# A transformer block on one core: ScalarE copies 192 score pieces as bf16, VectorE joins them three at a time

## The reference, cut to what matters

```
mod = (silu(c) @ wmod).reshape(4, 6, 1, 256)          # sa, ca, ga, sb, cb, gb
h = layernorm(x) * (1 + ca) + sa                      # x: 4 x 1024 x 256
q, k, v = 16 heads of 16 from h @ w_qkv.T + b_qkv
attn = softmax(q @ k.T / 4);  vals = attn @ v
x = x + ga * (vals @ w_o.T + b_o)
h = layernorm(x) * (1 + cb) + sb
scores = sigmoid(h @ gate.T); pick 6 of 32 experts out of 4 of 8 groups; weights = 2.5 * normalised scores
x = x + gb * (sum over chosen experts of weight * expert(h) + shared_expert(h))
```

## Time and profile before

| | |
|---|---|
| timed runs | 1418.58 us median of 3 (1416.19 to 1419.35) |
| span of the profiled execution | 1412.3 us |
| TensorE matmul busy | 1342.8 us (95%) |
| VectorE busy | 1134.9 us (80%) |
| ScalarE busy | 753.7 us (53%) |
| attention steps | 152.3 to 880.3 us |

### The profile page before, as it was taken

One profiled execution on the slowest core, in us unless ns is written; L12 is line 12 of the kernel. 1 busy time (PEld: TensorE's weight loads), 2 busy tenths in 40 slices (PEclk: granted clock), 3 DMA queues, 4 the chain that ended last, 5 costly groups with the idle time before them and its releaser, 6 DMA issues.

```text
span 1412.3 us, 30839 instructions
## 1 busy us (share of the span) xinstructions
PE 1342.8 (95%) x8191; PEld 672.8 (48%) x8192; DVE 1134.9 (80%) x2823; ACT 753.7 (53%) x1155; POOL 606.9 (43%) x782
## 2 busy tenths in 40 slices
PE   7997999999999999999999999999999999999895
PEld 4552222332333323323333232568788888888551
DVE  7886999999999999999999994566566656656588
ACT  3762477676767676777677768113343433334100
POOL 4000113143644534636346357527755555655300
PEclk9997799999999999999999999999999999999999
DMA  6898355533546345444464355947766665666698
GB/s 218 260 270 216 93 171 133 121 85 83 125 126 156 91 121 149 132 96 107 125 170 117 105 155 176 274 136 234 231 199 206 202 183 177 180 179 178 238 344 337
DMA packets 216958, 243.55 MB, mean 172 GB/s; under 512 B 93948, under 2 KB 181500, under 8 KB 216736
## 3 DMA queue, kind: packets, MB, share of 16 engines
q1 hardware_dynamic: 189328, 166.42, 43.6%
q0 software_dynamic: 21776, 68.07, 13.4%
q10 hardware_dynamic: 5760, 7.87, 1.7%
HBM read 133.98 MB, written 108.28 MB: 172 GB/s over the span
## 4 chain that ended last, share of the span: by engine, by line
PE 71%; DVE 13%; DMA 4%; issue 1%; SPq 1%; ACT 1%; POOL 0%; DVEq 0%; POOLq 0%
PE psO L1174 14%; PE ex_psGU L1682 13%; PE psE L1161 13%; PE psM L1151 9%; DVE piece_max L1048 9%; PE ex_psY L1697 7%; PE ex_psX L1671 3%; PE psM L505 2%; PE ex_psA L1691 2%; PE psGU L1495 1%; DMA wide<-results 1%; PE co_psS L1951 1%; PE late_psGU L1931 1%; PE late_psX L1942 1%; PE psM L524 1%
## 5 line engine op out<-in xcount | busy, mean ns | idle before, releaser
L1048 DVE TENSOR_REDUCE piece_max<-psM 128x1 f32<-128x512 f32 x1024 | 641.9, 680 | 27.3 <-PE psM L1151 24.0
L1115 ACT ACTIVATE wide<-psE 128x1024 f32<-128x1024 f32 x512 | 496.8, 1021 | 206.2 <-PE psE L1161 204.1
L1151 PE MATMUL psM<-wide 48*128 48x512 bf16 x1024 | 324.0, 395 | 19.9 <-DVE piece_max L1048 11.7
L1161 PE MATMUL psE<-wide 49*128 49x512 bf16 (+1 forms) x2048 | 328.7, 380 | 3.2 <-DMA wide<-maxima 2.8
L1763 POOL DMA_INDIRECT results<-vals_inv,places x223 | 213.9, 959 | 150.5 <-DVE vals_inv L1749 86.4
L1174 PE MATMUL psO<-wide 128*32 128x512 f32 x2048 | 273.6, 606 | 0.6 <-ACT wide L1115 0.6
L1151 PEld LDWEIGHTS psM<-wide 48*128 48x128 bf16 x1024 | 78.1, 93 | 348.1 <-DVE piece_max L1048 277.3
L1682 PE MATMUL ex_psGU<-wide,ex_xT 128*128 x892 | 231.3, 382 | 0.8 <-ACT ex_xT L1714 0.7
L1161 PEld LDWEIGHTS psE<-wide 49*128 49x128 bf16 (+1 forms) x2048 | 117.6, 95 | 92.3 <-issue 8.7
L1682 PEld LDWEIGHTS ex_psGU<-wide,ex_xT 128*128 128x128 f32 x892 | 152.1, 190 | 14.6 <-issue 2.3
L1714 ACT ACTIVATE ex_xT<-ex_psX 128x256 f32<-128x256 f32 x223 | 85.3, 383 | 121.3 <-PE ex_psX L1671 118.5
(11 more groups left out here) (281 smaller groups left out, 1262.8 us busy)
## 6 DMA issues: line engine op xcount, KB each, us to landing
wide<-qk_parts SPq DMA_DIRECT2D x384, 64.0 KB
wide<-results SPq DMA_DIRECT2D x16, 1536.0 KB, 9.5
rows<-lists SPq DMA_DIRECT2D x112, 160.0 KB
h2Ts<-lists SPq DMA_DIRECT2D x111, 160.0 KB
qk_parts<-parts SPq DMA_DIRECT2D x32, 384.0 KB, 3.1
xin<-in_x_dram SPq DMA_DIRECT2D x16, 512.0 KB, 4.2
v_values<-vst SPq DMA_DIRECT2D x32, 256.0 KB, 3.5
wide<-v_values SPq DMA_DIRECT2D x16, 512.0 KB
```

What stands on the lines that cost most here:

```text
L1048: v.tensor_reduce(piece_max[:, qh, (x * PAIRS + h) * KT // QH + qt, kh:kh + 1], bank_of("piece", PIECES * group + n), AX.X, ALU.max, negat ...
L1115: nc.scalar.activation(probs[:, step % 2, 2 * pair:2 * pair + 2], psE[:, pair], ACT.Exp, scale=HD ** -0.5).then_inc(exp_ok, 1)
L1151: nc.tensor.matmul(bank_of(*user), qa[g][rows, h, qt * P:(qt + 1) * P], ka[g][rows, h, kh * 512:(kh + 1) * 512], start=True, stop=True).th ...
L1161: mm = nc.tensor.matmul(psE[:, pair, x], k[g][part, pair, kt * P:(kt + 1) * P], q[g][part, pair, qh * 512:(qh + 1) * 512], start=(q is qa) ...
```

## The change

ScalarE now reads six pieces of each half of 32, 192 in all: always p2, in the steps that are 0, 1, 2, 4, 5 and 6 of the half (`held_at`; step 0 of a half is step 5 modulo 8). `hold` copies such a piece as bf16 to SBUF, at the end of ScalarE's step. VectorE leaves these pieces out and works on three copies at a time in `join`: elementwise maximum of 3x256 elements (level 0), of 3x128 (level 1), of 3x64 (level 2), and a reduction of 3x64 to three maxima (level 3). The first three are joined in step 4 of the half, the second three in the first step of the next half, where `finish` now stands too, behind p1 and ahead of p3. `divide` moves from step 5 to step 6 of a group. The maxima are stored with one transfer and loaded with one, and `max_d` has a part for each half.

```diff
-DIVIDE = 5
+DIVIDE = 6
+    HELD_PIECE, HELD_STEPS, TRIPLE = 2, (0, 1, 2, 4, 5, 6), 3
+    FIRST_JOINED = 4
...
+        held = [of.bitcast(BF16)[:, 0:TRIPLE * 512].rearrange("p (n k) -> p n k", n=TRIPLE)
+                for of in (env.act_s[:].rearrange("p m t -> p (m t)"),
+                           env.x2[:, TPC * LAST:].rearrange("p i d -> p (i d)"))]
...
+        def held_at(n):
+            return n % 4 == HELD_PIECE and n // 4 % STEPS_HALF in HELD_STEPS
...
             def store_max(k):
-                at = COLS * (k % QH)
                 sp.wait_ge(max_ready, k + 1)
-                for n in range(P // 32):
-                    sp.dma_start(env.max_d[at:at + COLS, n], neg_max_t[32 * n + at:32 * n + at + COLS, :]
-                                 ).then_inc(max_stored, 16)
+                sp.dma_start(env.max_d[k % QH].rearrange("c n r -> n c r"), neg_max_t[:]).then_inc(max_stored, 16)
...
+            def join(half, triple, level):
+                of = held[triple]
+                if level < 3:
+                    width = 256 >> level
+                    if level == 0:
+                        dve.wait_ge(piece_held, TRIPLE * (2 * half + triple + 1))
+                    else:
+                        chain.ready()
+                    chain.then(v.tensor_tensor(of[:, :, 0:width], of[:, :, 0:width], of[:, :, width:2 * width], ALU.max))
+                else:
+                    chain.ready()
+                    at = HELD_STEPS[TRIPLE * triple]
+                    v.tensor_reduce(piece_max[:, half % QH, at:at + TRIPLE, HELD_PIECE // 2], of[:, :, 0:64], AX.X, ALU.max,
+                                    negate=True).then_inc(joined, 1)
+
+            def piece_or_join(group, n):
+                if not held_at(n):
+                    piece_maximum(group, n)
+                p, r = n // 4 % STEPS_HALF, n % 4
+                if p == FIRST_JOINED:
+                    for level in ((0,), (1, 2), (3,), ())[r]:
+                        join(QH * group + n // HALF_PIECES, 0, level)
+
+            def finish_half(k, n):
+                if n == 0:
+                    join(k, 1, 0)
+                elif n == 1:
+                    for level in (1, 2, 3):
+                        join(k, 1, level)
+                elif n == 2:
+                    finish(k)
...
                 for n in range(4):
                     beside(step, n)
                     if group < NGR:
-                        piece_maximum(group, first + n)
-                if group < NGR and (first + 4) % HALF_PIECES == 0:
-                    finish(QH * group + first // HALF_PIECES)
+                        piece_or_join(group, first + n)
+                    done = QH * group + first // HALF_PIECES - 1
+                    if first % HALF_PIECES == 0 and 0 < done < QH * NGR:
+                        finish_half(done, n)
...
+            def hold(group, n):
+                at = held_before(PIECES * group + n)
+                triple, slot = divmod(at, TRIPLE)
+                act.wait_ge(piece_done, PIECES * group + n + 1)
+                if slot == 0:
+                    wait(act, joined, triple - 1)
+                nc.scalar.activation(held[triple % 2][:, slot], bank_of("piece", PIECES * group + n), ACT.Copy
+                                     ).then_inc(piece_held, 1)
...
+                to, first = pieces_for(step)
+                for n in range(first, first + 4):
+                    if to < NGR and held_at(n):
+                        hold(to, n)
...
-                if c == "piece":
-                    pe.wait_ge(piece_read, w + 1)
+                if c == "piece" and held_at(w % PIECES):
+                    pe.wait_ge(piece_held, held_before(w + 1))
+                elif c == "piece":
+                    pe.wait_ge(piece_read, read_before(w + 1))
```

More of the change, by code:

```diff
@@ L736, in attention_phase @@
     PAIRS = HG // 2
+    STEPS_HALF = HALF_PIECES // 4
+    HELD_PIECE, HELD_STEPS, TRIPLE = 2, (0, 1, 2, 4, 5, 6), 3
+    FIRST_JOINED = 4
     NGR = B * NG
@@ L780, in chunk_at, with held_before, read_before @@
             return c - 1, w
+        def held_at(n):
+            return n % 4 == HELD_PIECE and n // 4 % STEPS_HALF in HELD_STEPS
+        def held_before(n):
+            halves, n = divmod(n, HALF_PIECES)
+            return len(HELD_STEPS) * halves + sum(held_at(m) for m in range(n))
+        def read_before(n):
+            return n - held_before(n)
         ring = Ring(HALF_PIECES, PIECES * NGR)
@@ L786, in bank_of @@
             return psM[:, ring.bank[user]] if user in ring.bank else None
+        env.pieces_read = read_before(PIECES * NGR)
         def pieces_for(step):
@@ L794, in store_max @@
             def store_max(k):
-                at = COLS * (k % QH)
                 sp.wait_ge(max_ready, k + 1)
-                for n in range(P // 32):
-                    sp.dma_start(env.max_d[at:at + COLS, n], neg_max_t[32 * n + at:32 * n + at + COLS, :]
-                                 ).then_inc(max_stored, 16)
+                sp.dma_start(env.max_d[k % QH].rearrange("c n r -> n c r"), neg_max_t[:]).then_inc(max_stored, 16)
             def load_max(k):
                 group, qh = divmod(k, QH)
-                g, each = group % NG, COLS // 2
-                sp.wait_ge(max_stored, 4 * 16 * (k + 1))
-                for x in range(2):
-                    at = HALF * x + QROWS
-                    sp.dma_start(qa[g][at:at + 1, :, qh * S // QH:(qh + 1) * S // QH],
-                                 env.max_d[qh * COLS + x * each:qh * COLS + (x + 1) * each]
-                                 .rearrange("(h q) n r -> h (q n r)", h=PAIRS).unsqueeze(0)).then_inc(max_there, 16)
+                g = group % NG
+                sp.wait_ge(max_stored, 16 * (k + 1))
+                sp.dma_start(qa[g][QROWS:QROWS + HALF + 1:HALF, :, qh * S // QH:(qh + 1) * S // QH],
+                             env.max_d[k % QH, qh * COLS:(qh + 1) * COLS]
+                             .rearrange("(x h q) n r -> x h (q n r)", x=2, h=PAIRS)).then_inc(max_there, 16)
             def put_max(k):
@@ L1053, in finish @@
                 cols = slice(COLS * (k % QH), COLS * (k % QH + 1))
-                dve.wait_ge(piece_read, HALF_PIECES * (k + 1))
+                dve.wait_ge(piece_read, read_before(HALF_PIECES * (k + 1)))
+                dve.wait_ge(joined, 2 * (k + 1))
                 chain.link(v.tensor_tensor(neg_max[:, cols], part[:, :, 0], part[:, :, 1], ALU.min))
-                wait(dve, max_stored, 4 * 16 * k)
+                wait(dve, max_stored, 16 * k)
                 v.transpose(neg_max_t[:], neg_max[:]).then_inc(max_ready, 1)
@@ L1075, in _ @@
             for n in range(HALF_PIECES):
-                piece_maximum(0, n)
+                piece_or_join(0, n)
             dve.wait_ge(env.zeroed, 1)
-            finish(0)
+            for n in range(3):
+                finish_half(0, n)
             for fixed in (env.gmax[:, :, GROUPS:], env.masked[:, :, E:], env.gkeys[:], env.keys[:]):
@@ L1108, in beside @@
                     half_scores(act, env, c, bank_of(c, w))
+            def hold(group, n):
[6 more added lines that the diff above has]
+                                     ).then_inc(piece_held, 1)
+            for n in range(HALF_PIECES + 4 * AHEAD):
+                if held_at(n):
+                    hold(0, n)
             for step in range(ALL):
@@ L1200, in _ @@
                 if s % KT == 0:
-                    pe.wait_ge(max_there, 2 * 16 * (step // KT + 1))
+                    pe.wait_ge(max_there, 16 * (step // KT + 1))
                 to, first = pieces_for(step)
@@ L2002, in declare @@
     env.v_d = dram("v_values", (B, NG, P, KT, HG * 2 * HD), F32)
-    env.max_d = dram("maxima", (HG * KT, P // 32, 32), BF16)
+    env.max_d = dram("maxima", (QH, HG * KT, P // 32, 32), BF16)
     env.o_d = dram("o_sums", (B, H, HD, HD, S // HD), F32)
```

6 lines of the change are left out of this document (3 added, 3 removed).

## The result

The changed kernel takes 1494.01 us (median of 5 runs, 1483.24 to 1501.41), the kernel before 1419.35 (5 runs, 1416.19 to 1422.24). The ratio is 1.0519, 95% interval 1.0496 to 1.0541. The forecast was slower, 1450.7, at most 1494. So the direction was right and the size was less than half of what came: +31 forecast, +75 measured. The runs also spread over 18 us, where those of before spread over 6. The trace is of the fastest of the five, 1483.24 us: what the median has more than that, 11 us, no trace shows. A ratio compares only runs within 1.5% of the fastest of their kernel, which leaves out two runs of the kernel with strided joins and one of the kernel before with its pieces further ahead.

A forecast was written before the change was run, and what follows sets the result against it. TensorE bounds plain steps, with VectorE close; bursts beyond three banks' lead cost time. Six windows 26.4, last 3.0, first 32 steps 4.7, start -2: +32 us, span 1444, runs 1450.7; range 1416 to 1494.

The forecast's parts named there:

- What bounds the kernel, and the ring: Plain steps are TensorE's; it runs only three banks ahead, so over 2.49 us of VectorE work in a step costs at once.
- Price of a join: VectorE per triple: levels 0.55, 0.35, 0.25 us and reduction 0.34 (low end), or 0.96, 0.55, 0.35, 0.34 (high end).
- Rival 1: VectorE's joins stream one element a cycle, each 0.70 us dearer, 59 in the steps: +41, 1492 us; chance 0.15.
- Joins in step 1 modulo 8: First triple's joins, at w (step within a 32-step window) = 1, 9, 17: TensorE waits 0.22 and 0.32, together +0.54 us.
- the sum: All terms together: 4.4 us a window, 26.4 for six; whole kernel +32 us, span 1444, runs 1450.7.
- Joins and finish in step 5 modulo 8: Second triple's joins plus finish delay TensorE by 1.00 us, or 1.42 with division; about +0.8 net each.
- ScalarE in w = 21 to 23: Copy of p2 queues behind the routing reading, next p0 waits: +0.84 us twice, 0.5 behind the gate; +1.6 net.
- Maxima: Row of maxima arrives 0.7 us later, nearly always covered by the joins' stall; otherwise this wait costs about 0.3 a half.
- The start: Ahead of step 0: 6 reductions fewer (-3.6), joins +2.8, transfers -1.2, together -2 us.
- The small terms: Late in a window: w = 11 and 12, small waits go, -0.2 us; w = 25 to 31, fewer reductions against joins, -0.2.
- the last window: The final window, whose pieces end at w = 20: +3.0 us.
- the first 32 steps: Attention steps without routing: 4 x 0.54 + 4 x 0.65 = 4.7 us more.

The follow-up runs named there:

- the last versions: Joins spread over three steps, pieces further ahead, every fourth half's second triple unjoined: ratios 1.002, 1.0035, 1.0017 with an earlier finish, 1.0038 without, against the kernel before.

## Why the prediction was wrong in its size

**What bounds the kernel, and the ring: right.** Bursts count, not sums alone. Spreading the joins takes 30 us off with the same work in them, most of it by the bursts.

**Price of a join: right, at the low end, where nothing stands beside it.** 546, 346 and 258 ns, 354 for the reduction. The strided joins give the other end. Rival 1, with the high end, would have given 1492, nearly what was measured, by a mechanism that the trace refutes. A time that fits is no evidence for its story.

**Joins in step 1 modulo 8: right where nothing stood beside them, and here the forecast failed.** In the window from step 160, w = 2 and 3 take 2.86 and 2.63, together 0.51 more than two steps of 2.49, against 0.54. But the step took this price at every place. It never asked what GpSimd does at the time, though the multiplication was in its own rows, for another purpose, and w = 9 and 10 were among its places. There the join takes 3.15 us and the two steps 4.4 us more than without the meeting. So GpSimd is the term that the sum had at nothing: in the trace the five meetings at w = 10 cost 24.1 us and the two long joins of the first routing window 6.8 (w = 2 to 4), together 31 of the 37 us by which its span of 1481.5 exceeds the forecast's 1444. The wait added to GpSimd takes 33 us off in the medians, where the forecast misses 43.

**The clock: no term for it.** TensorE's clock was taken as constant. Of the 4.4 us of a meeting 2.5 are the stall; the rest is lost at the 1.2 GHz level behind it. Where the clock did not fall, a stall of 2.14 cost 2.4 in all. In the trace of the changed kernel the clock stood at 1.2 GHz for 41 us between steps 3 and 255, in the one before never.

**Joins and finish in step 5 modulo 8: right.** Forecast 3.5 to 3.9 for the step behind; w = 6 takes 3.76, with the division behind its finish; w = 14, without, takes 3.36, 0.1 below.

**ScalarE in w = 21 to 23: right.** Forecast steps of 3.8, 5.1 and 2.9, measured 3.90, 5.22 and 2.90; w = 21 to 24 take 1.7 us more than before, against a net of 1.6, and undoing it gives 1.4.

**Maxima: put at nothing, too small.** The stall was to cover them. This is the timeline of the changed kernel behind the finish of w = 6, in the window from step 160:

```profile
675.97 0.57 SPq L817 DMA_DIRECT2D maxima<-neg_max_t  x1
...
677.94 0.54 SPq L823 DMA_DIRECT2D wide<-maxima  x1
...
680.89 0.61 PE L1230 MATMUL psE<-wide 49*128 49x512 bf16 x4 [0.53 <-DMA wide<-maxima]
```

The load lands after TensorE wants it, w = 7 takes 3.32 us and not 2.63: 0.7 in five windows, 0.3 to 0.4 in the first and the last. "If the stall goes, this wait is next" was right: it is 0.2 to 1.5 us without joins.

**The start: wrong.** 2 us were to be saved ahead of step 0. It begins at 152.14, before at 152.26. Without the joins it begins at 148.22, so they cost 3.9 us there and not 2.8; and the single transfers alone save nothing of the 1.2 (152.88).

**The small terms.** w = 11 and 12 were to give back 0.2 us and give back nothing; w = 25 to 31 were to give back 0.2 and cost 0.3 (22.0 us against 21.7, window from step 160).

With the multiplication out of the way the runs are 10 us above the sum (1460.6 against 1450.7). The traces are further apart than the runs, 45.6 us in the spans against the sum's 32, and say where: the first routing window, where two long joins are left, is 6.8 above its term (104.6 - 93.4 = 11.2, not 4.4); the five windows behind it are 7.2 above theirs, 3.5 of that by the maxima; the start is 1.9 above, the last window 0.3, and the first 32 steps are 2.9 below theirs.

## What to carry to other kernels

Before work is moved onto VectorE as operations with two inputs in SBUF, look up in the trace what GpSimd does in the same microseconds: an operation that took 0.35 us on its own took 3.15 here beside a neighbour of 2.37, and a duration from one place of the trace does not hold at another. If an engine is fed by three buffers, put new work into the gaps that the old work left, one piece to a gap. Price a stall of some microseconds on TensorE with what the clock may take behind it: here 1.9 us on top of 2.5 where it fell, 0.3 on top of 2.1 where it did not. And compare traces with medians before a gain is put down to a cause: here the traced run was 11 us faster than the median.

## What the runs showed of the hardware

A VectorE join with two SBUF inputs, 0.35 us long on its own, took 3.15 us beside a GpSimd TENSOR_TENSOR recorded as 2.37 us long and as beginning 0.56 us after the join did; by these records the join should have been over first. Either GpSimd holds VectorE off for longer than its recorded span, or that span is rough. Beside a TENSOR_SCALAR of GpSimd of 1.2 us joins took at most 0.24 us more in this trace, and reductions out of PSUM beside either kept their 0.68.

After 4 us in which TensorE was busy for 1.26 us, the granted clock was 0.50 for 3.4 us; after 4 us in which it was busy for 1.65 us, in the run with the copy first (678 to 682), it stayed at 1.00. In the kernel before it never fell between step 3 and the experts.

The kernel before took 1418 us in some pairs and 1539 in others, and chip 12 was in a pair of either kind. In the pairs at 1539, TensorE, VectorE and ScalarE stood still together for 0.4 to 2.3 us at w = 22, 23 and 26 of the windows in the traces of the last versions, without a semaphore to explain it, and in the first of them the experts took 99 us longer than in the trace of the spread joins. What they wait for I have not shown.
